# A limit of two on the indirect scatters under way, and the last pages summed per token by 0/1 matrices on TensorE

## The reference, cut to what matters

```python
# second mixture, for all T = 2048 tokens
topk_idx, topk_w = _router(x, gate_w, e_bias)        # (T, 6), (T, 6)
y = sum over k of topk_w[:, k] * (_relu2(x @ up_w[topk_idx[:, k]].T) @ down_w[topk_idx[:, k]].T)
x = x + y + shared(x)
```

## Time and profile before

| | us |
|---|---|
| median of 3 runs | 889.14 |
| lowest and highest | 884.67, 889.75 |
| the profiled execution | 888.47 |
| its span in the profile | 886.6 |
| mean granted TensorE clock | 0.903 of full |

### The profile page before, as it was taken

The page is one execution under the profiler, slowest core; times in us unless marked ns, Lnnn a source line. Parts: engine busy times, 40 slices in busy tenths (PEclk is TensorE's granted clock), DMA queues, the critical chain, the costliest instruction groups (busy, mean ns, idle before and its releaser), DMA issues.

```text
span 886.6 us, 14153 instructions
## 1 busy us (share of the span) xinstructions
PE 722.6 (82%) x4526; PEld 631.4 (71%) x4526; DVE 416.7 (47%) x1615; ACT 273.0 (31%) x620; POOL 308.5 (35%) x322
## 2 busy tenths in 40 slices
PE   3868886389999999999899888866776868787865
PEld 2647776289999999999899877533456757676754
DVE  4998664022333243546644742725104444456563
ACT  2636631022111111222223122321123455445540
POOL 1333307600010111100552354172712656556560
PEclk9898859589999999999999998796978899989998
DMA  8999992231776767755866624242646556587866
GB/s 257 396 296 268 257 252 97 102 125 53 231 231 219 218 221 244 246 169 190 304 218 232 217 89 170 92 166 87 217 154 189 177 158 191 164 288 243 285 215 250
DMA packets 93534, 181.22 MB, mean 204 GB/s; under 512 B 9857, under 2 KB 54998, under 8 KB 93182
## 3 DMA queue, kind: packets, MB, share of 16 engines
q1 hardware_dynamic: 78048, 138.67, 50.9%
q0 software_dynamic: 13344, 38.68, 11.6%
q10 hardware_dynamic: 2046, 2.71, 1.0%
HBM read 134.07 MB, written 65.62 MB: 225 GB/s over the span
## 4 chain that ended last, share of the span: by engine, by line
PE 56%; DVE 16%; issue 10%; another core or an unknown queue 6%; DMA 4%; ACT 3%; POOL 3%; SPq 1%; DVEq 0%; POOLq 0%; ACTq 0%
PE PB L618 16%; PE PB L655 11%; PE PB L632 5%; PE PB L825 4%; PE PB L816 4%; PE PB L763 3%; POOL rows_out L1930 3%; PE PB L777 2%; PE PB L804 2%; DMA X<-in_x 2%; PE PB L684 1%; PE PB L600 1%; DMA MEM<-rows_out 1%; DVE WK L1256 1%
## 5 line engine op out<-in xcount | busy, mean ns | idle before, releaser
L618 PE MATMUL PB<-XT,MEM 128*128 128x128 f32 x1584 | 185.9, 276 | 1.1 <-issue 1.1
L618 PEld LDWEIGHTS PB<-XT,MEM 128*128 128x128 f32 x1584 | 181.7, 193 | 1.5 <-issue 1.3
L1882 POOL DMA_INDIRECT sorted_y<-WK x36 | 34.5, 958 | 279.0 <-DVE WK L1470 279.0
L1891 POOL DMA_INDIRECT rows_in<-MEM x96 | 93.5, 974 | 65.1 <-DVE MEM L1674 36.6
L655 PE MATMUL PB<-MEM,WK 128*128 x432 | 99.7, 380 | 3.3 <-DVE MEM L1646 1.9
L825 PE MATMUL PB<-MEM,WK 128*128 x228 | 67.6, 424 | 32.0 <-DVE WK L1823 26.1
L655 PEld LDWEIGHTS PB<-MEM,WK 128*128 128x128 f32 x432 | 79.3, 190 | 13.2 <-issue 3.9
L1930 POOL DMA_INDIRECT rows_out<-WS,MEM x58 | 56.7, 977 | 64.4 <-ACT WS L1045 49.2
L825 PEld LDWEIGHTS PB<-MEM,WK 128*128 128x128 f32 x228 | 42.2, 207 | 41.2 <-issue 36.9
L1930 POOL DMA_INDIRECT rows_out<-MEM x56 | 56.2, 1003 | 40.5 <-ACT MEM L1045 25.7
L939 ACT ACTIVATE XT<-PB 128x256 f32<-128x256 f32 x52 | 19.8, 381 | 162.2 <-PE PB L600 134.2
(11 more groups left out here) (280 smaller groups left out, 1255.4 us busy)
## 6 DMA issues: line engine op xcount, KB each, us to landing
MEM<-in_w SPq DMA_DIRECT2D x36, 896.0 KB
rows_in<-in_consts SPq DMA_DIRECT2D x32, 600.0 KB, 12.2
MEM<-in_w SPq DMA_DIRECT2D x36, 512.0 KB
MEM<-rows_in SPq DMA_DIRECT2D x58, 300.0 KB
MEM<-rows_out SPq DMA_DIRECT2D x16, 768.0 KB, 7.0
MEM<-in_w SPq DMA_DIRECT2D x32, 256.0 KB, 2.8
MEM<-in_w SPq DMA_DIRECT2D x2, 3072.0 KB, 18.9
sorted_x<-MEM SPq DMA_DIRECT2D x1, 5070.0 KB, 39.7
```

Of the source, the lines that this page charges most:

```text
L618: t = e.matmul(o[:, to:to + P], UPW[m][i % (3 - m)][:, k, c * P:(c + 1) * P], XT[:, n % 2, k, :], start=(k == 0), stop=(k == 1))
L1882: e.indirect_dma_start(out=DY, out_offset=bass.IndirectOffsetOnAxis(ap=DEST[:, i:i + 1], axis=0), in_=YS[:, i % 2, :], in_offset=None).the ...
L1891: e.indirect_dma_start(out=DX1, out_offset=bass.IndirectOffsetOnAxis(ap=SLOT1[:, i, j:j + 1], axis=0), in_=XR[:, i, :], in_offset=None).th ...
```

## The change

It has two parts.

**At most two scatters under way.** Each scatter of L1873, each of `rows_out` and each of L1930 first waits for the landing of the scatter two before it in its own series. The first two series use two semaphores by parity (`sent0`, `sent1`; `rows0`, `rows1`) instead of four by group. The `sorted_y` scatters have no such wait.

**The last pages by TensorE.** `OWN = (6 * 12 + 32) // 2 = 52`. Pages of pairs 0 to 51 are scattered as before. For pairs 52 and up, ACT writes the scaled pages to four buffers `YO`; DVE compares each page's `PT6` with a row of 512 constants (`TOKENS`, the first row number of each token of group 3), which gives a 128 x 512 matrix of 0 and 1 (`HOT`); and PE multiplies it with the page, 4 matmuls of 128 x 128 by 256 columns a page, accumulated over all these pages in PSUM banks 6 and 7. Up matmuls use banks 4 and 5 alone from pair 50 on. Nothing is scattered for these pages, so the `rows_out` region of group 3 is zeroed before (4 DMAs from SP in the expert blocks). Loads of tiles 8 to 15 (`fetch6`) now wait for page 103. POOL sums the even tiles from 8 (4 adds each), DVE the odd ones; DVE adds the PSUM banks to tiles 12 to 15 (`total`); SP stores tiles 8 to 11, ACT 12 to 15. PE's identity sums are gone. The DVE sums of tiles 6 and 7 move from steps 54 and 56 to 53 and 54.

```diff
+OWN = (TOPK * GB[3] + E1) // 2
-FETCH6 = {31: 0, 33: 1, 35: 2, 37: 3, 43: 4, 45: 5, 47: 6, 49: 7, 55: 8, 56: 9}
+FETCH6 = {31: 0, 33: 1, 35: 2, 37: 3, 43: 4, 45: 5, 47: 6, 49: 7}
+def up_bank(s):
+    return 4 + s % (4 if s < OWN - 2 else 2)
 # PE
+            def to_tokens(s, n_pairs):
+                q.wait_ge("by", s)
+                q.wait_ge("hot", s)
+                q.wait_ge("bh", OWN - 3)
+                for b in (2 * s, 2 * s + 1):
+                    last = b == 2 * n_pairs - 1
+                    for i in range(4):
+                        t = e.matmul(PB[:, 6 + i // 2, i % 2 * D:(i % 2 + 1) * D], HOT[b % 4][:, i * P:(i + 1) * P], YO[b % 4],
+                                     start=(b == 2 * OWN and i % 2 == 0), stop=last, skip_group_check=True)
 ...
+                if OWN <= s - 2 < n_pairs:
+                    to_tokens(s - 2, n_pairs)
 ...
-                for i in range(8, NT, 2):
-                    o = PB[:, i // 2, 0:D]
 ...
 # DVE
+            def one_hot(s):
 ...
+                for b in (2 * s, 2 * s + 1):
+                    t = e.tensor_scalar(HOT[b % 4], TOKENS, PT6[:, s // 2 % 2, b % 4:b % 4 + 1], None, ALU.is_equal)
 ...
                 for i in range(9, NT, 2):
                     whole(sum_rows(i))
+                    if i > GB[3]:
+                        h = (i - GB[3]) // 2
+                        q.wait_ge("sv", i)
+                        q.wait_ge("sp", i - 1)
+                        q.wait_ge("owned", h)
+                        e.tensor_tensor(X[:, i - 1:i + 1, :], X[:, i - 1:i + 1, :],
+                                        PB[:, 6 + h, :].rearrange("p (t d) -> p t d", t=2), ALU.add).then_inc(
 # POOL
                 for k in range(2):
+                    q.wait_ge(f"sent{k}", i - 1)
                     e.indirect_dma_start(
 ...
+                    if i or j > 1:
+                        q.wait_ge(f"rows{j % 2}", i if j > 1 else i - 1, (j - 2) % TOPK)
                     e.indirect_dma_start(
 ...
-                if 0 <= s - 2 < n_pairs:
+                if 0 <= s - 2 < OWN:
 ...
                     for b in (2 * r, 2 * r + 1):
+                        q.wait_ge(f"yb{(b - 2) % 16}", b - 2)
                         e.indirect_dma_start(
 ...
+            for i in range(8, NT, 2):
+                y = Y6[place(i)]
+                q.wait_ge(f"l6_{place(i)}", i)
+                e.tensor_tensor(y[:, 0:3 * D], y[:, 0:3 * D], y[:, 3 * D:6 * D], ALU.add).then_inc(*q.mark("set1"))
 ...
 # SP
+                if i in (6, 8, 10, 12):
+                    lo = TRASH + (GB[3] + i // 2 - 3) * P * TOPK
+                    e.dma_start(DY1[lo:lo + P * TOPK, :].rearrange("(p n) d -> p n d", p=P),
+                                ZERO[:, 0:D].unsqueeze(1).broadcast_to([P, TOPK, D])).then_inc(*q.land("zeroed1", i))
 ...
-                upto = 6 * GB[GROUP[i] + 1] + 31
-                upto = upto if upto < 112 else 2 * pairs - 1
+                upto = min(TOPK * GB[GROUP[i] + 1] + E1, 2 * OWN) - 1
 ...
+            for i in range(8, NT):
+                fetch6(i)
```

More of the change, by code:

```diff
@@ L91 @@
     "first_slots": ("mm", "pr0", "slot0", "tab"),
-    "mid_sums": ("t1", "wi", "t2", "ro", "rank", "pages"),
+    "mid_sums": ("t1", "wi", "t2", "ro", "rank", "pages", "own", "owned"),
     "mid_copies": ("q1", "xp", "q2", "xta", "sc"),
@@ L826, in down2 @@
                 t.then_inc(*q.mark("bd", s))
+            def to_tokens(s, n_pairs):
[7 more added lines that the diff above has]
+                                     start=(b == 2 * OWN and i % 2 == 0), stop=last, skip_group_check=True)
+                        if last and i == 1:
+                            t.then_inc(*q.mark("owned", 0))
+                t.then_inc(*(q.mark("owned", 1) if last else q.mark("own", s)))
             def step(s, n_pairs):
@@ L1065, in end1 @@
                     step(s, n_pairs)
-                for i in range(8, NT, 2):
-                    q.wait_ge("sum", i)
-                    e.activation(X[:, i, :], PB[:, i // 2, 0:D], ACT.Copy).then_inc(*q.mark("end", i))
-                    q.wait_ge("end", i)
-                    q.wait_ge("sv", i + 1)
+                for h in range(2):
+                    i = GB[3] + 2 * h
+                    q.wait_ge("total", h)
                     e.dma_start(od[:, i:i + 2, :], X[:, i:i + 2, :]).then_inc(*q.land("out_b", i))
@@ L1932, in step @@
                             in_=YB[b // 8 % 2][:, b % 8, :], in_offset=None).then_inc(*q.land(f"yb{b % 16}", b))
-            for s in range(-1, COMMON):
+            q.wait_ge("zeroed1", 12)
+            for s in range(-1, OWN + 2):
                 step(s, 58)
-            def end1(c):
-                n_pairs = PAIRS[c]
-                for s in range(COMMON, n_pairs + 2):
-                    step(s, n_pairs)
-            q.copies(number1, [2 * n for n in PAIRS], end1)
+            for i in range(8, NT, 2):
+                y = Y6[place(i)]
+                q.wait_ge(f"l6_{place(i)}", i)
+                e.tensor_tensor(y[:, 0:3 * D], y[:, 0:3 * D], y[:, 3 * D:6 * D], ALU.add).then_inc(*q.mark("set1"))
+                for k in (1, 2):
+                    q.wait_ge(*q.last)
+                    e.tensor_tensor(y[:, 0:D], y[:, 0:D], y[:, k * D:(k + 1) * D], ALU.add).then_inc(*q.mark("set1"))
+                q.wait_ge(*q.last)
+                q.wait_ge("drn", GROUP[i])
+                e.tensor_tensor(X[:, i, :], X[:, i, :], y[:, 0:D], ALU.add).then_inc(*q.mark("sp", i))
         def sp_program(q):
@@ L1974, in fetch @@
                 if kind == "b":
-                    for g in range(NG):
-                        q.wait_ge(f"sent{g}", 4 * g + 3, 1)
+                    for k in range(2):
+                        q.wait_ge(f"sent{k}", NT - 1)
                     q.wait_ge("tab")
@@ L2060, in fetch1 @@
                 q.wait_ge("wi", NR - 1, 1)
-                for g in range(NR):
-                    q.wait_ge(f"rows{g}", GB[g + 1] - 1, TOPK - 1)
+                for j in range(2):
+                    q.wait_ge(f"rows{j}", NT - 1, TOPK - 2 + j)
                 q.wait_ge("bt", s - 6)
@@ L2102, in sp_program @@
                 fetched = step(s, 58, fetched)
+            store(6)
+            for i in range(8, NT):
+                fetch6(i)
             def end1(c):
                 n_pairs, k = PAIRS[c], fetched
-                for s in range(COMMON, n_pairs + 2):
+                for s in range(COMMON, n_pairs):
                     k = step(s, n_pairs, k)
-                for i in range(10, NT):
-                    fetch6(i, n_pairs)
+                for i in (8, 10):
+                    store(i)
             q.copies(number1, [2 * n for n in PAIRS], end1)
-            q.wait_ge("out_a", 6)
+            q.wait_ge("out_a", 10)
             q.wait_ge("out_b", NT - 2)
```

66 lines of the change are left out of this document (43 added, 23 removed).

## The result

The changed kernel takes 904.88 us (median of 5 runs, 898.32 to 910.17), the kernel before on the same chip 889.75 (884.67 to 896.01): a ratio of 1.017, interval 1.0123 to 1.0217. It is 1.7% slower. Ratios leave out runs more than 1.5% above the fastest of their kernel, so they can differ a little from the quotient of the medians. The profiled execution of the kernel after took 898.32 us with a span of 896.4, that of before 888.47 with 886.6.

A forecast was written before the change was run, and what follows sets the result against it. PE, busy 82% of the span, was seen losing time while POOL scatters back to back. 888.47 + 4 upstream + 8.8 pages - 7.6 tail = 893.7, plus 0.67 for the median: 894 us, range 848 to 911.

The forecast's parts named there:

- the forecast's own case: Whole kernel: 894 us, range 884 to 904 for landings in the pages of 3.0 to 3.4 us; chance 0.38.
- slower by more: Whole kernel: outcome slower than the 880.2 to 898.0 that counts as the same; chance 0.29.
- I see no row by which the same spacing would release PE. So I take the stalls as unchanged.: First mixture and rows of groups 2 and 3: PE's stalls stay; the limit itself costs +1 us in the first mixture.
- it frees it in part: Rival, 870 us: PE's signals pass in POOL's pauses among other transfers, nothing changes in quiet bursts; chance 0.17.
- Upstream costs, +4: Before the pages: the limit adds 1 us in the first mixture, 2 in groups 2 and 3, 1 in the expert blocks.
- The pages, "one landing time + 0.28", 3.48 a pair: Pages 0 to 103: landing of 3.2 us plus 0.28 a pair, 177.5 us against 168.7, +8.8.
- the third rival: Pages: POOL becomes the bound once landings exceed 3.03 us, 915 us in all; chance 0.15.
- The tail, -7.6: From page 103's load to the end: eight tile loads set the pace, end at 879.0 instead of 886.6.
- PE in the last pairs, zeroing, constants, moved sums: Pairs 52 to 56: matmuls add 4 us a pair to PE's 2.25; zeroing, constants and moved sums cost nothing.
- What would show it: Signs in the changed profile: PE tiles of 4.2 us through the burst, page interval over 190 (177 forecast), tail 26.6 us.
- the first rival: First mixture and rows: the limit frees PE wholly by keeping POOL's queue empty, 845 us in all; chance 0.19.

The follow-up runs named there:

- e3: Kernel before plus the limit of two scatters under way in sorted_x, rows_in and rows_out: 893.30 us against 776.89, ratio 1.1492.
- e12: Kernel before plus a 0.3 us memset before every second sorted_x scatter, limit of three in rows_in, none in rows_out: 862.84 us against 892.63, ratio 0.9686.
- e4: Kernel before plus the limit of two for sorted_x and rows_in alone: 809.78 us against 776.89, ratio 1.0404.
- e11: Changed kernel with all limits, tiles 8 to 15 summed by DVE alone, without POOL's sums: 884.87 us, ratio 1.1399 to the kernel before (777.05).
- e7: Changed kernel without any limit, tiles 8 to 15 summed by DVE alone: 900.23 us against 896.55 for the kernel before, ratio 1.0042.
- e2: Changed kernel without any limit, keeping the token sums by TensorE: 780.02 us against 776.89 for the kernel before, ratio 1.0035.
- e9: Kernel before plus a limit of two for sorted_x, three for rows_in, none for rows_out: 789.92 us against 777.05, ratio 1.0175.
- e5: Kernel before, unchanged, traced on another chip where its median is 896.55 us: 902.35 us in one run.
- e10: Kernel before, no limit, plus a 0.3 us memset on POOL before every second scatter of sorted_x and rows_in: 779.20 us against 777.05, ratio 1.0025.

## Why the prediction was right in the number and wrong on the way

The median of 904.88 lies inside the stated 848 to 911, 10.9 us above the forecast of 894. It lies just outside the 884 to 904 that the forecast's own case allowed, in the part called "slower by more", which had a chance of 0.29. The working had +4 upstream, +8.8 in the pages and -7.6 in the tail, and the profiled run has -28.3, +40.1 and -2.0. Three terms were wrong and nearly cancelled, so that the number came out near is luck.

- **"I see no row by which the same spacing would release PE. So I take the stalls as unchanged."** This step failed. I had the right place and symptom (PE idle by "issue" in back-to-back scatters), counted scatters under way, found two in either kernel and called the limit idle, at 0.025 us a scatter. The spacing isn't the same: 1.45 instead of 1.28, 0.17 us a scatter. The landing of 2.3 was too short: in e3 a scatter of `sorted_x` lands after 2.44 us in the median and 2.74 in the mean, and with these landings and 0.27 us to the next start its burst comes to 48.2 us, as measured (129.82 to 177.99). With the limit PE works 16.5 of the 23.7 us that it lost in the window (44.8 - 28.3 against 52 - 28.3). By e12 the spacing alone gives back only a part of it. The rival "it frees it in part" had its mechanism backwards as well, since it expected gains only where landings are long; the first mixture, in quiet, gained 14.6.
- **Upstream costs, +4.** In the rows the burst of 24 scatters grew from 29.1 to 40.1 us. I put this at +2, on the ground that "most of these scatters run in quiet". Once PE is freed nothing hides it: PE stands for 27.2 us until the rows of group 3 are there, so part of what was freed went back at once. On a chip that doesn't hold up PE only this cost is left: +33 (e4).
- **The pages, "one landing time + 0.28", 3.48 a pair.** The mechanism was right, the third rival's: POOL is the bound. The landing was right too, 3.2 for the 3.17 of e3, whose pages take 206.9 us (its last packets end 2.74 us after the start in the mean, those of the kernel after 2.82). Mis-sized was what a pair pays beside it. With the landings of e3 as they came, 0.27 us behind each and at least 1.26 between two starts, the pages come to 185.2 us instead of the forecast 177.5, because the mean of unequal landings hides the waits that the long ones cause. With the measured 0.75 at the first of a pair they come to 204.6. So the wake at the first of a pair is the largest missing term, some 19 us. By the Trainium skill, DMA: Bandwidth & Descriptors, Anatomy of one DMA, 131 KB come to an estimated 2.3 us (2.0 and the bytes by its 436 GB/s). The median of 2.49 is near it, and yet the limit wasn't free, because a chain of waits pays the long landings and the wake as well.
- **The tail, -7.6.** The order was right (loads, then sums, then one add from PSUM; PE done at 862, ahead of the loads). Two prices were missing: "beside the loads" took DVE at the earlier trace rows and POOL at the earlier trace rows, each measured without the other, and nothing stood for POOL's closing. By the Trainium skill, SBUF — State Buffer, section "SBUF: two separate sides", a DVE instruction with two inputs in SBUF and a GpSimd one that reads SBUF exclude each other for the whole instruction. The rows bear it out: 0.83 for 0.42 and 2.23 for 0.96, and back to 0.42 and 0.95 in e11; the DVE add that starts at 872.82 ends 0.81 us after POOL's add of 768 columns does (875.05 and 874.24), so nearly all its work lies behind POOL's. I had POOL's adds on the page and did not ask what they do to DVE. A tile cost POOL 5.06 us, where I had allowed it at most 4.4.
- **PE in the last pairs, zeroing, constants, moved sums.** Right as far as the runs tell: a group of 16 records of `to_tokens` takes 3.72 us (4 forecast), a last pair of e7 5.5 from one group to the next (6.25 forecast), and without limits the second half of the change measures as +0.35 and +0.42% (e2, e7).
- **What would show it.** I had written that PE running through the burst would mean the first rival, and over 190 us in the pages the third. Both came at once. The prediction priced each alone, and gave no chance to the two together, which is what happened: 845 + (208.7 - 177.5) = 876 would have been its number, still 29 under the measured, since only 28 of the 50 us of stalls came through and 2 of the tail's 7.6.

## What to carry to other kernels

A limit on transfers under way does two things at once: it thins the issuing engine's stream, which may free others, and it can make an item pay a landing and a wake-up. Put it where the issuing engine has time to spare (the first mixture and the rows on a chip of this sort), loosen it until the burst isn't the bound (three instead of two gave 0.9775; e12, with pauses in the first mixture, three for the rows and none in the pages, came to 0.9686), and leave it out where that engine is next to the bound. Read a wake-up at the place where it will be paid before it is multiplied by 51: 0.27 us held for a DMA's landing in three places and 0.75 in the fourth. Run a chain of waits with the single landings and not with their mean; and when work is shared between DVE and GpSimd, look at what each costs while the other runs, and at who is last at the end of the program.

## What the runs showed of the hardware that I had not expected

- The same kernel takes a median of 777 us on some occasions and of 890 to 897 on others, each steady within 2% on its chip (772.89 to 779.69 in 13 runs, 890.58 to 904.6 in 19). In the second case back-to-back GpSimd scatters hold up PE (26.8 to 28.3 of 52 us busy), in the first they don't (50.7 in e2). The record names the same chip number for e9 to e11 and for e12, one of each sort, so it may be a state rather than a specimen. What it is remains open; so the change is worth +1.7% and +0.3% on two chips of one sort, and on the other its limits alone cost 14.9% (e3), and the change with DVE's tail 14.0% (e11). No kernel here beat 777 there.
- The two sorts can be told from a trace by its records of landings. With some 93,530 DMA packets each, the traces of the kernel before hold 5029 such records (before) and 5091 (e5), that of e10, the same kernel with pauses, 9076. `prof` then gives no time to landing for the scatters, here before and e3:

```profile
rows_out<-WS,MEM POOLq DMA_INDIRECT x58
rows_out<-WS,MEM POOLq DMA_INDIRECT x58, 2.4
```

  In the kernel before, "issue" and "remote" can therefore stand for a releaser whose record is missing. PE's holes are not missing instructions: all three traces have 4526 matmuls. Every run on record has a span and a clock, so none shows what the kernel takes without being recorded, and whether the recording has a part in holding up PE stays open.
- PE is released by degrees: with scatters every 1.27 us it works 19.1 of 39.6 us of the burst (e5), with 1.27 and 1.45 in turn through pauses 29.1 of 43.5 (e12), with waits for landings at about that pace 37.6 of 45.1 (after). Which part of the machine they share wasn't found.
- A scatter that waits for a DMA's landing starts 0.27 us after it in `sorted_x`, in `rows_in` and at the second of a pair in the pages, but 0.75 at the first of a pair (e3). Before that scatter stand two more waits, for ACT and for DVE; whether they are the difference wasn't tried.
- POOL's closing instruction runs for 8.7 us beyond its last sum (887.48 to 896.16), and as long beyond its last scatter in e7, but 5.3 us in the kernel before (865.39 to 870.67) and 2.2 in e3. Ending with POOL costs the kernel after 5.2 us of its span.
